# A fused attention and expert layer on one core: new order at the start, tanh for sigmoid, packed shared rows, attention added on GpSimd

## What is computed

```python
x = x + layernorm(attn(layernorm(x), W_basis, W_v, b_v, W_o, b_o))
x = x + layernorm(ffn(layernorm(x), gate_w, gate_bias, Wg, Wu, Wd, Sg, Su, Sd))

def attn(h):
    latent = h @ W_basis.T                       # queries and keys are the same, R = 64
    v = h @ W_v.T + b_v
    att = softmax(causal(latent @ latent.T / sqrt(R)))
    return (att @ v) @ W_o.T + b_o

def ffn(x):
    scores = sigmoid(x @ gate_w.T)               # 64 experts in 8 groups
    choice = scores + gate_bias                  # 4 groups by their two best, then the top 8
    rw = 2.5 * chosen scores / their sum
    routed = sum over e of rw[:, e] * ((silu(x @ Wg[e].T) * (x @ Wu[e].T)) @ Wd[e].T)
    shared = (silu(x @ Sg.T) * (x @ Su.T)) @ Sd.T   # 176 rows
    return routed + shared
```

## Time and profile before

| what | us |
|---|---|
| median of three runs (lowest, highest) | 492.09 (491.2, 492.85) |
| the profiled execution | 490.94 |
| its span | 489.1 |
| busy in it: PE, PEld | 453.5, 368.0 |
| busy in it: DVE, ACT, POOL | 331.1, 292.3, 340.8 |

### The profile page before, as it was taken

One profiled execution on the slowest core, in us unless ns is written; L12 is line 12 of the kernel. 1 busy time (PEld: TensorE's weight loads), 2 busy tenths in 40 slices (PEclk: granted clock), 3 DMA queues, 4 the chain that ended last, 5 costly groups with the idle time before them and its releaser, 6 DMA issues.

```text
span 489.1 us, 8048 instructions
## 1 busy us (share of the span) xinstructions
PE 453.5 (93%) x2144; PEld 368.0 (75%) x2144; DVE 331.1 (68%) x712; ACT 292.3 (60%) x570; POOL 340.8 (70%) x324
## 2 busy tenths in 40 slices
PE   0799886889999999999999999999999999999994
PEld 0598774658677888888888888888888888887894
DVE  4466798778556666666666666666666666666786
ACT  1478988665656555655555565655555556555652
POOL 6473556767468767677777777777777776778675
PEclk9999999799999999999999999999999999999998
DMA  7000000100001101010000101010101010100011
GB/s 199 1 2 2 17 18 0 33 2 0 1 16 35 33 17 32 17 30 18 20 29 16 32 16 32 16 32 16 32 16 32 16 32 16 28 4 0 0 45 43
DMA packets 12297, 11.58 MB, mean 24 GB/s; under 512 B 1734, under 2 KB 12278, under 8 KB 12278
## 3 DMA queue, kind: packets, MB, share of 16 engines
q1 hardware_dynamic: 11414, 11.02, 7.9%
q10 hardware_dynamic: 864, 0.33, 0.3%
HBM read 10.30 MB, written 1.05 MB: 23 GB/s over the span
## 4 chain that ended last, share of the span: by engine, by line
PE 82%; POOL 5%; DVE 4%; issue 4%; ACT 3%; DMA 1%; ACTq 0%; POOLq 0%; DVEq 0%
PE ps L1257 24%; PE ps L1259 24%; PE ps L1258 24%; POOL lat_hi L510 3%; PE ps L1209 3%; PE ps L1195 1%; DMA bo_sb<-in_b_o 1%; PE ps L1147 1%; PE ps L1155 1%; PE ps L1393 1%; PE ps L1175 1%; PE ps L1176 1%; PE ps L1252 1%; ACT L691 1%; POOL rstd L487 0%
## 5 line engine op out<-in xcount | busy, mean ns | idle before, releaser
L510 POOL TENSOR_TENSOR lat_hi<-hid,lat_hl 128x512 fp32r<-128x512 f32 (+1 forms) x188 | 241.2, 1285 | 101.9 <-ACT lat_hl L729 101.5
L960 DVE TENSOR_TENSOR up_w<-ps,route_w 128x512 f32<-128x512 f32 (+1 forms) x180 | 122.2, 679 | 107.8 <-PE ps L1259 107.6
L719 ACT ACTIVATE ps<-ps 128x512 f32<-128x512 f32 (+1 forms) x180 | 103.0, 573 | 132.8 <-PE ps L1259 132.3
L1257 PE MATMUL ps<-x_hi,w_hi 128*128 128x512 f32 (+1 forms) x360 | 141.0, 392 | 3.5 <-POOL w_lo L518 2.0
L1259 PE MATMUL ps<-x_hi,w_lo 128*128 128x512 f32 (+1 forms) x360 | 140.4, 390 | 0.0
L1258 PE MATMUL ps<-x_lo,w_hi 128*128 128x512 f32 (+1 forms) x360 | 140.1, 389 | 0.0
L970 DVE TENSOR_TENSOR hid<-ps,up_w 128x512 f32<-128x512 f32 (+1 forms) x180 | 122.4, 680 | 11.1 <-ACT ps L719 2.9
L729 ACT CAST lat_hl<-hid 128x512 fp32r<-128x512 f32 (+1 forms) x188 | 113.6, 605 | 16.0 <-DVE hid L970 12.6
L1257 PEld LDWEIGHTS ps<-x_hi,w_hi 128*128 128x128 f32 x360 | 67.8, 188 | 20.1 <-POOL w_lo L518 2.4
L1259 PEld LDWEIGHTS ps<-x_hi,w_lo 128*128 128x128 f32 x360 | 67.9, 189 | 14.8
L1258 PEld LDWEIGHTS ps<-x_lo,w_hi 128*128 128x128 f32 x360 | 67.9, 189 | 14.3
(11 more groups left out here) (132 smaller groups left out, 387.2 us busy)
## 6 DMA issues: line engine op xcount, KB each, us to landing
w_raw<-in_w_experts SPq DMA_DIRECT2D x44, 192.0 KB, 2.4
x_sb<-in_x SPq DMA_DIRECT2D x3, 256.0 KB, 6.0
out<-x_sb SPq DMA_DIRECT2D x3, 256.0 KB, 2.3
sh_raw<-in_w_shared_up SPq DMA_DIRECT2D x2, 88.0 KB
x_sb<-in_x ACTq DMA_DIRECT2D x2, 64.0 KB, 2.3
x_sb<-in_x SPq DMA_DIRECT2D x2, 64.0 KB, 2.1
out<-x_sb SPq DMA_DIRECT2D x1, 128.0 KB, 1.8
out<-x_sb SPq DMA_DIRECT2D x2, 64.0 KB, 1.6
```

Of the source, the lines that this page charges most:

```text
L510: g.tensor_tensor(hid_lo[:, k % DEEP, 0:w], hid[:, k % 2, 0:w], hid_hi[:, k % DEEP, 0:w], ALU.subtract).then_inc(s_hlo, 1)
L719: a.activation(bank, bank, ACT.Silu).then_inc(s_gated, 1)
L960: v.tensor_tensor(up_w[:, k % 2, 0:w], ps[:, gate_bank(k) + 1, 0:w], route_w[:, group, 512 * q + lo:512 * q + lo + w], ALU.mult).then_inc( ...
L1257: t_.matmul(out_, hi, mhi, start=start, stop=False)
```

## The change

- Orders: all eight lists are new. At the start the first transposes and the latent of quad 0 come before the weight product K0 (PE and ACT), P0 comes right behind S0 on DVE, and the centring is in two parts: B0 for the output weights, which waits for three transfers, and B1 for the bias, which has a semaphore of its own. PE begins with ten products of the identity with itself. POOL makes the select tables (B0) behind P1.
- SP loads gate weights and bias between x quads 1 and 2.
- Shared rows: the 176 rows are cut 128 + 48 instead of 88 + 88. The second step keeps up and gate in one weight block, the gate columns from 64 on, so that three products give both (`rest_gate_up`); seven transfers instead of four, and a memset of the gap.
- Sigmoid is Tanh with scale 0.5 on ACT, and DVE turns it into 0.5 * t + 0.5 (F on DVE) before POOL's bias sum.
- `add_attention` moves from DVE (four fused instructions) to POOL (a product with the root broadcast, then a sum, each over the whole quad).
- The picked scores come in one DVE pass: (left == TAKEN) * scores; keep_experts and POOL's weigh_scores go.
- In the tail DVE makes the last low hidden part (W20), and ACT takes the square root of the last unit's variance (Y4, with a Sqrt of a constant column before it, P0); DVE inverts it in N4.

Left out below: the new semaphores, the helpers that count steps and waits (`ups_through`, `is_rest`), the copies of the packed weights in L on ACT and POOL (now 384 columns in one for c = 0, and 112 columns plus 48 rows for c = 1), the row counts handed to Z and W, and the dispatch of stages.

```diff
-            "K0 P0 Q0 V0 P1 A00 A01 A02 Q1 T00 T02 A03 C00 T04 C01 T06 A10 C02 C03 A11 T10 T11 "
-            "V1 A12 T12 P2 C10 A13 T13 Q2 C11 T14 P3 V2 A20 T15 Q3 T16 T17 C12 C13 A21 W0 E0 "
-            "A22 T20 V3 F0 A23 T22 C20 A30 T24 A31 C21 T26 A32 T30 C22 T31 C23 T32 C30 T33 E1 "
-            "A33 T34 C31 T35 F1 T36 T37 G0 W1 Z0 C32 N00 C33 E2 F2 Z1 Z2 N01 Z3 G1 W2 Z4 W3 E3 "
-            "W4 F3 Z5 Z6 N10 W5 N11 G2 Z7 W6 W7 N20 Z8 Z9 W8 N21 Z10 Z11 W9 Z12 Z13 W10 W11 "
-            "Z14 W12 W13 Z15 W14 G3 Z16 N30 W15 W16 Z17 Z18 N31 W17 W18 Z19 Z20 W19 W20 Z21 "
-            "Z22 W21 W22 Z23 "
+            "P0 Q0 K0 V0 A00 P1 A01 T00 Q1 A02 A03 T02 C00 T04 C01 T06 A10 C02 C03 A11 W0 T10 "
+            "T11 A12 V1 P2 A13 T12 C10 T13 Q2 C11 P3 V2 A20 T14 T15 Q3 T16 T17 C12 T20 C13 A21 "
+            "E0 A22 V3 F0 A23 C20 T22 T24 A30 C21 T26 C22 A31 T30 C23 T31 A32 T32 T33 A33 C30 "
+            "E1 T34 F1 C31 T35 T36 G0 Z0 T37 C32 N00 E2 C33 F2 W1 Z1 N01 Z2 G1 Z3 W2 Z4 E3 W3 "
+            "Z5 W4 F3 Z6 N10 N11 G2 W5 Z7 W6 W7 N20 Z8 W8 N21 Z9 Z10 Z11 W9 Z12 Z13 W10 Z14 "
+            "W11 W12 W13 Z15 G3 Z16 W14 N30 W15 W16 Z17 Z18 N31 W17 W18 Z19 W19 Z20 Z21 W20 "
+            "W21 Z22 W22 Z23 "
         )
         ACT_ORDER = stages(
-            "P0 K0 Q0 P1 A00 A01 T00 Q1 A02 T02 A03 T04 C01 T06 R0 A10 C03 T10 A11 T12 A12 P2 "
-            "L0 Q2 C11 P3 T14 A13 Q3 T16 A20 Y0 C13 E0 F0 A21 T20 A22 T22 A23 T24 A30 C21 T26 "
-            "A31 T30 R1 C23 Y1 A32 T32 L1 E1 T34 A33 F1 T36 G0 C31 Z0 Y2 N00 E2 C33 Z1 F2 N01 "
-            "Z2 G1 W0 Z3 W1 R2 R3 W2 Y3 Z4 W3 E3 F3 Z5 W4 Z6 N10 N11 W5 G2 Z7 W6 N20 W7 Z8 Z9 "
-            "W8 N21 Z10 W9 Z11 W10 W11 Z12 Z13 W12 W13 Z14 Z15 W14 G3 W15 Z16 N30 Z17 W16 Z18 "
-            "W17 N31 Z19 W18 Z20 W19 Z21 W20 Z22 W21 R4 Z23 W22 R5 "
+            "P0 Q0 K0 A00 P1 A01 T00 Q1 A02 T02 A03 T04 C01 T06 A10 C03 A11 T10 P2 T12 A12 R0 "
+            "L0 L1 Q2 C11 A13 P3 T14 A20 Q3 T16 T20 Y0 C13 E0 A21 F0 A22 T22 A23 C21 T24 A30 "
+            "T26 R1 T30 C23 A31 Y1 A32 T32 E1 T34 F1 A33 C31 Z0 T36 G0 Y2 N00 E2 F2 C33 Z1 N01 "
+            "Z2 R2 W0 W1 Z3 G1 R3 Y3 W2 E3 Z4 W3 W4 Z5 F3 Z6 N10 N11 W5 G2 W6 Z7 N20 Z8 W7 N21 "
+            "W8 Z9 Z10 W9 Z11 W10 W11 Z12 Z13 W12 W13 Z14 Z15 G3 Z16 W14 W15 N30 W16 Z17 Z18 "
+            "W17 N31 W18 Z19 W19 Z20 Z21 W20 W21 Z22 R4 Z23 W22 R5 "
         )
         DVE_ORDER = stages(
-            "S0 S1 B0 P0 K0 V0 Q0 A00 A01 S2 A02 A03 Q1 S3 A10 A11 V1 T11 A12 U0 T13 A13 Q2 X0 "
-            "T15 V2 A20 T17 Q3 A21 A22 U1 V3 A23 H0 A30 X1 A31 J0 T31 A32 I0 T33 O0 M0 A33 U2 "
-            "T35 X2 T37 G0 H1 J1 Z0 I1 O1 Z1 M1 U3 H2 X3 Z2 J2 Z3 G1 I2 O2 Z4 Z5 M2 Z6 G2 Z7 "
-            "H3 Z8 Z9 J3 Z10 Z11 I3 Z12 O3 Z13 M3 Z14 Z15 G3 Z16 Z17 Z18 Z19 Z20 Z21 Z22 Z23 "
+            "S0 P0 B0 S1 B1 K0 Q0 A00 V0 A01 S2 A02 A03 Q1 S3 A10 A11 T11 V1 A12 A13 T13 Q2 X0 "
+            "A20 T15 V2 T17 Q3 A21 V3 A22 F0 A23 H0 A30 X1 A31 J0 T31 A32 T33 I0 A33 O0 M0 F1 "
+            "T35 X2 T37 G0 H1 J1 Z0 I1 O1 F2 M1 Z1 H2 X3 Z2 J2 Z3 G1 I2 O2 Z4 Z5 M2 Z6 F3 G2 "
+            "Z7 H3 Z8 J3 Z9 Z10 Z11 Z12 Z13 I3 O3 M3 Z14 Z15 G3 Z16 Z17 Z18 Z19 Z20 Z21 Z22 "
+            "Z23 "
         )
         POOL_ORDER = stages(
-            "S0 S1 P1 S2 S3 P2 D0 P3 X0 L0 D1 F0 X1 J0 R0 D2 E0 O0 L1 M0 E1 R1 F1 X2 J1 E2 O1 "
-            "D3 F2 M1 W0 X3 R2 W1 W2 J2 R3 W3 F3 E3 O2 M2 W4 W5 W6 W7 W8 J3 W9 W10 W11 W12 O3 "
-            "W13 M3 W14 W15 W16 W17 W18 W19 W20 W21 R4 W22 R5 "
+            "S0 S1 P1 B0 S2 S3 P2 P3 D0 U0 R0 L0 X0 D1 U1 F0 X1 D2 R1 J0 E0 L1 U2 M0 E1 F1 X2 "
+            "J1 E2 D3 F2 U3 M1 R2 W0 W1 X3 J2 R3 W2 W3 W4 M2 W5 F3 W6 W7 W8 W9 J3 W10 W11 E3 "
+            "W12 M3 W13 W14 W15 W16 W17 W18 W19 W20 W21 R4 W22 R5 "
...
-            "D0 Z0 D1 D2 Z1 Z2 D3 Z3 Z4 D4 Z5 D5 Z6 D6 Z7 Z8 D7 Z9 T0 Z10 D8 D9 D10 Z11 D11 "
-            "Z12 T1 Z13 Z14 D12 D13 D14 Z15 Z16 T2 Z17 D15 D16 Z18 Z19 D17 D18 D19 T3 D20 D21 "
-            "D22 T4 "
+            "D0 Z0 D1 Z1 D2 Z2 D3 Z3 Z4 D4 D5 Z5 D6 Z6 Z7 T0 Z8 D7 D8 Z9 Z10 D9 D10 Z11 T1 Z12 "
+            "D11 D12 D13 Z13 Z14 D14 Z15 Z16 T2 D15 D16 Z17 D17 D18 Z18 Z19 T3 D19 D20 D21 D22 "
+            "T4 "
         )
         ACT_TAIL = stages(
-            "W0 R2 Z0 W1 R3 Z1 Z2 W2 W3 Z3 W4 Z4 W5 Z5 W6 Z6 W7 Z7 Z8 O0 W8 Z9 W9 Z10 W10 O1 "
-            "Z11 W11 Z12 W12 Z13 W13 Z14 W14 O2 Z15 Z16 W15 W16 Z17 W17 W18 Z18 Z19 O3 W19 W20 "
+            "R2 W0 Z0 W1 R3 Z1 Z2 W2 Z3 W3 W4 Z4 W5 Z5 W6 Z6 O0 Z7 W7 W8 Z8 W9 Z9 W10 Z10 O1 "
+            "Z11 W11 Z12 W12 W13 Z13 Z14 W14 O2 W15 Z15 Z16 W16 Z17 W17 Z18 W18 Z19 O3 W19 W20 "
+            "P0 Y4 "
         )
         DVE_TAIL = stages(
-            "Z0 Z1 Z2 Z3 Z4 Z5 Z6 Z7 Z8 Z9 S0 Z10 N0 Z11 Z12 S1 Z13 Z14 N1 Z15 Z16 Z17 S2 Z18 "
-            "Z19 N2 S3 O4 S4 N3 N4 "
+            "Z0 Z1 Z2 Z3 Z4 Z5 Z6 Z7 S0 Z8 Z9 Z10 N0 Z11 Z12 S1 Z13 Z14 Z15 Z16 S2 Z17 N1 Z18 "
+            "Z19 S3 W20 O4 N2 S4 N3 N4 "
         )
         POOL_TAIL = stages(
-            "W0 R2 W1 R3 W2 W3 W4 W5 W6 W7 W8 W9 Y0 W10 W11 W12 W13 Y1 W14 W15 W16 W17 W18 Y2 "
-            "W19 W20 Y3 Y4 "
+            "R2 W0 W1 R3 W2 W3 W4 W5 W6 W7 Y0 W8 W9 W10 W11 W12 W13 W14 W15 Y1 W16 W17 W18 W19 "
+            "Y2 Y3 "
...
-            for q in range(1, QUADS):
+            def load_quad(q):
                 sp.dma_start(x_sb[:, 4 * q:4 * q + 4, :],
                              x_tiles[:, 4 * q:4 * q + 4, :]).then_inc(s_x[q], 16)
+
+            load_quad(1)
             sp.dma_start(gw_sb[:], gate_w_t).then_inc(s_gwl, 16)
             sp.dma_start(gb_sb[:], gate_bias.to_broadcast([P, E])).then_inc(s_gwl, 16)
-            for c in range(SHARED):
-                sp.dma_start(sh_raw[:, c, 0:2 * SROWS], w_shared_up[c]).then_inc(s_shl, 16)
-                sp.dma_start(sh_raw[0:SROWS, c, WD:WD + P], w_shared_down[c]).then_inc(s_shl, 16)
+            load_quad(2)
+            load_quad(3)
+            own = P - SROWS
+            ups = [w_shared_up[c].rearrange("h (g n) -> h g n", g=2) for c in range(SHARED)]
+            full = sh_raw[:, 0, 0:WD].rearrange("p (g n) -> p g n", g=2)
+            sp.dma_start(full[:, :, 0:SROWS], ups[0]).then_inc(s_shl, 16)
+            sp.dma_start(full[:, :, SROWS:P], ups[1][:, :, 0:own]).then_inc(s_shl, 16)
+            sp.dma_start(sh_raw[0:SROWS, 0, WD:WD + P], w_shared_down[0]).then_inc(s_shl, 16)
+            sp.dma_start(sh_raw[SROWS:P, 0, WD:WD + P],
+                         w_shared_down[1, 0:own]).then_inc(s_shl, 16)
+            sp.dma_start(sh_raw[:, 1, 0:REST], ups[1][:, 1, own:SROWS]).then_inc(s_shl, 16)
+            sp.dma_start(sh_raw[:, 1, GATE_AT:GATE_AT + REST],
+                         ups[1][:, 0, own:SROWS]).then_inc(s_shl, 16)
+            sp.dma_start(sh_raw[0:REST, 1, WD:WD + P],
+                         w_shared_down[1, own:SROWS]).then_inc(s_shl, 16)
...
+            g.memset(eps_col[:], EPS).then_inc(s_eps, 1)
+            g.memset(sh_raw[:, 1, REST:GATE_AT], 0.0).then_inc(s_gap, 1)
...
+            def add_attention(q):
+
+                k = 2 + q % 2
+                own = x1_sb[:, 4 * q:4 * q + 4, :]
+                pool.wait_ge(s_rstd, NORMS.index(("D", q)) + 1)
+                link(g.tensor_tensor(own, att[:, q % 2],
+                                     rstd[:, k].unsqueeze(2).to_broadcast([P, 4, C]), ALU.mult))
+                g.tensor_tensor(own, own, x_sb[:, 4 * q:4 * q + 4, :], ALU.add).then_inc(s_x1, 1)
...
-            def weigh_scores(q):
-
-                pool.wait_ge(s_kept, q + 1)
-                g.tensor_tensor(left[:], left[:], scores[:, q % 2], ALU.mult).then_inc(s_picked, 1)
...
-                    if (what, q) == ("S", 1):
-                        make_select()
...
-                             ACT.Sigmoid).then_inc(s_sc, 1)
+                             ACT.Tanh, scale=0.5).then_inc(s_sc, 1)
...
+                if is_rest(s):
+                    a.activation(gated[0:REST, k % 2, :], ps[GATE_AT:GATE_AT + REST, gate_bank(k), :],
+                                 ACT.Silu).then_inc(s_gated, 1)
...
+                elif what == "P":
+
+                    act.wait_ge(s_eps, 1)
+                    a.activation(deviation[:, 2:3], eps_col[:], ACT.Sqrt)
+                elif what == "Y":
+                    act.wait_ge(s_var, len(VARIANCES) + k + 1)
+                    a.activation(deviation[:, 0:2], mv[:, 2 + k % 2, 0:2, 1], ACT.Sqrt,
+                                 bias=eps_col[:]).then_inc(s_dev, 1)
...
-            def add_attention(q):
-
-                k = 2 + q % 2
-                dve.wait_ge(s_rstd, NORMS.index(("D", q)) + 1)
-                for t in range(4):
-                    ins = v.scalar_tensor_tensor(
-                        out=x1_sb[:, 4 * q + t, :], in0=att[:, q % 2, t, 0:C],
-                        scalar=rstd[:, k, t:t + 1], in1=x_sb[:, 4 * q + t, :],
-                        op0=ALU.mult, op1=ALU.add)
-                ins.then_inc(s_x1, 1)
...
+            def sigmoid_of_tanh(q):
+
```

(78 more changed lines are left out.)

107 lines of the change are left out of this document (66 added, 41 removed).

## The result

The kernel after takes 485.03 us, median of 4 runs (483.34 to 485.48), against 492.47 for the kernel before beside it: ratio 0.9848, 95% interval 0.9817 to 0.9879. It is 7.4 us faster. The forecast was 475.6 us, range 469.0 to 482.5; the result lies outside it, at less than half of the forecast gain. The profiled run took 483.34 us, 1.84 us more than its span as before, so the traces differ by 7.6 us, and can be compared term by term. It is the fastest of the four, 1.7 us under their median.

The account below looks back on a forecast made before the run. TensorE was taken to bind the loop from 147 to 442 us, so gains come only from the start, gaps to 147 us, fewer matmuls and the tail. Terms summed to 16.5 us: 492.09 - 16.5 = 475.6 us, range 469 to 482.5.

Parts of the forecast that it names:

- additions: Attention added on POOL: 1.5 us gained by relieving DVE, 1.5 us charged for POOL's fuller queue.
- The start: New order up to A01, with P1 as the limit and ten warming matmuls: 5.4 us gained, bounds 3.5 and 7.2.
- Tanh 1.8 us: Sigmoid by tanh drops table loads, ending TensorE's wait for exp_rows: 1.8 us gained, bounds 0 and 2.6.
- rival (c): Tanh is not in Silu's set, so four table loads stay in the middle: 478.2 us, chance 0.06.
- The middle: 75 to 94 us: half of 7.7 us of idle and slow-clock time goes, 4.0 us, bounds -3 and 7.7.
- rival (a): The middle keeps its gaps under another owner, POOL's pairs replacing DVE's pieces and table loads: 480.6 us, chance 0.25.
- Packing: Shared rows cut 128+48 save 12 matmuls of 0.231 us: 2.8 us, lower bound 1.4 if half falls into gaps.
- 94 to 147 us: Of 3.8 us TensorE idles from 94.2 to 147 us, 1.0 us goes, bounds 0 and 3.8.
- The tail: Shorter last root and earlier D22, less 0.35 us for N2's scalings: 1.5 us gained, bounds 0.5 and 2.5.
- 0.95 us for D22: In the tail, W19 ahead of the fourth root and W20 on DVE start D22 up to 1.3 us sooner; 0.95 taken.

Follow-up runs that it names:

- after_again: The kernel after, unchanged, measured once more in five rounds on one chip: 485.44 us (483.34 to 487.8).
- no_warm: The kernel after without the ten start matmuls that nobody reads: 485.82 us (484.88 to 486.46).
- rest_doubled: The kernel after with the packed gate-and-up products of each quad's 48 shared rows issued twice, 12 matmuls more: 487.22 us (484.76 to 488.56).
- the probe: The kernel after plus 18 VectorE instructions behind its end, alone, then beside a GpSimd train: five with both inputs in SBUF took 5.40 instead of 1.59 us.
- u3_dve: The kernel after with only quad 3's attention addition moved from GpSimd back to VectorE: 481.55 us, repeated 484.18 us.

## Why the prediction was wrong

The direction was right and the size not: 16.5 us were forecast and 7.4 came, 7.6 in the traces. To share these out one needs places in TensorE's list that have the same stages ahead of them in both kernels. A01, the logits of quad 2 (F2), N20 and the first step of the rounds are such places (20.33, 74.39, 98.15 and 142.79 us before; 14.55, 68.61, 92.20 and 135.93 after).

```profile
74.39 1.08 PE L1228 MATMUL ps<-gw_sb,x_t 128*128 128x64 f32 x8 [0.77 <-ACT x_t L684]
```

In the kernel after:

```profile
68.61 1.00 PE L1292 MATMUL ps<-gw_sb,x_t 128*128 128x64 f32 x8
```

| TensorE's work | gained, us | forecast, us |
|---|---|---|
| up to A01 | 5.8 | 5.4 |
| A01 to F2 | 0.0 | 1.8 (tanh), 1.5 - 1.5 (additions) |
| F2 to N20 | 0.2 | 4.0 (middle), 0.7 (3 packed matmuls) |
| N20 to the rounds | 0.9 | 1.0 (gaps), 2.1 (9 packed matmuls) |
| the tail | 0.7 | 1.5 |

- **The start, 5.4 us: right.** P1's transposes are at 14.16 (14.2 to 14.7 forecast) and A01 at 14.55 instead of 20.33, 5.8 us. But this trace has the best start; after_again's is 1.1 us worse at quad 2. Typical is 4.7.

```profile
8.90 1.13 PE L1211 MATMUL ps<-xn_t,wb_sb 128*128 128x512 f32 x2 [0.68 <-ACT xn_t L671]
...
14.16 0.63 PE L1175 MATMUL ps<-ident,xn 128*128 128x128 f32 x4 [1.24 <-POOL xn L575]
14.55 0.36 PE L1239 MATMUL ps<-lat_hi,lat_hl 128*128 128x256 f32 x1
```

The latent pair takes 1.13 instead of 2.07 us after the ten extra products; no_warm says how little of it reached the end.

- **Tanh 1.8 us: nothing of it between A01 and F2,** which are 54.06 us apart in both kernels. Taken back there alone it costs 1.7 us, and the additions 2.7, so both have a worth in the new order, but the order as a whole gained nothing over the old one here. Three table loads are left, as said, and rival (c) is out:

```profile
L671 ACT ACT_TABLE_LOAD x1 | 1.3, 1283 | 3.6 <-issue 3.6
L774 ACT ACT_TABLE_LOAD x1 | 1.3, 1283 | 0.0
L848 ACT ACT_TABLE_LOAD x1 | 1.3, 1283 | 0.0
```

- **The middle, 4.0 us: this step failed, the largest of the misses.** The busy times from F2 to N20, before and after:

```profile
74.39:98.15 23.76, 17.15 (x72) 12.76 (x72) 17.94 (x70) 18.18 (x34) 16.97 (x19) 0.86 0.06 17
```

```profile
68.61:92.20 23.59, 16.98 (x70) 12.04 (x69) 21.91 (x76) 12.58 (x29) 17.33 (x19) 0.86 0.06 18
```

TensorE idles 6.6 us in both and has the same mean clock: no gap closed, each only changed its owner, and the three packed matmuls are lost in the wait at N01. This is rival (a)'s picture. In after_again the same stretch takes 25.78 us, 2.0 us longer than before, at a clock of 0.74 from 75 to 95 us. I took half of the gaps as closed because the table loads vanish and GpSimd had idle time. GpSimd's idle time was what let H2 run in 2.2 us. Rival (a) named the mechanism, the lock between GpSimd and two-input VectorE instructions, and gave 480.6 us at 0.25; that too was 4.4 us low, as it kept the full tanh, packing and tail terms. I weighed the lock only as a slower add (0.53 us where two took 0.61) and not as a chain of eleven instructions of 0.2 us with a whole GpSimd instruction in front of each of six. That is 5.4 us on VectorE, of which 3.6 reached TensorE. The wait of 2.3 us at N01, from the new order and not from the lock, was not foreseen either. What was tried on the lock gave back 1.3 to 3.5 us of a miss of 9.4: it is shown as a cause, and as a part of the miss only.
- **The clock.** From 84.5 to 94.2 us it is 0.87 instead of 0.65, but 0.86 instead of 1.00 in the stretch ahead. In every trace of the new order with a wait of TensorE of 2.8 to 3.8 us in this stretch it fell behind that wait, whoever was awaited, so a wait of 3.6 us costs more than itself: behind it the matmuls come 0.43 us apart from 83.7 to 85 us instead of 0.23. Behind waits of 2.0 to 2.4 us it fell in some traces and not in others.
- **Packing, 2.8 us: 1.75.** The page has 2152 matmuls against 2144, which is 12 fewer and 20 extra ones at the start (ten products, two instructions each). By rest_doubled the nine behind N20 are worth 1.75 us and the three ahead of it nothing. The lower bound of 1.4 allowed for matmuls that fall into gaps; the sum took none.
- **94 to 147 us, 1.0 us: wrong.** From N20 to the rounds 0.9 us were gained, less than the nine matmuls alone are worth, so the gaps there cost about 0.8 us more than before.
- **The tail, 1.5 us: 0.7.** From the aggregate's end (478.05) to the last scaling's start is 0.63 us, as forecast, and 0.9 us are gained:

```profile
475.91 0.42 DVE L1111 TENSOR_TENSOR y_t<-ps,y_t 128x256 f32<-128x256 f32 x1 [0.71 <-PE ps L1323]
476.25 1.11 DVE L1134 SCALAR_TENSOR_TENSOR x_sb<-ps,rstd,x_sb 128x128 f32<-128x128 f32 x4
477.28 0.48 DVE L876 BATCH_NORM_STATS2 stats<-ps 128x6 f32<-128x128 f32 x2
477.80 0.25 DVE L879 BATCH_NORM_AGGREGATE mv<-stats 128x2 f32<-128x6 f32 x2
...
478.68 0.61 DVE L1134 SCALAR_TENSOR_TENSOR x_sb<-ps,rstd,x_sb 128x128 f32<-128x128 f32 x2
```

The 0.95 us for D22 was wrong: it starts at 475.25 instead of 482.13, just the 6.9 us of the loop. Before, its low parts ended at 482.08 on GpSimd; now the chain of hidden products ahead of it ends as late, and only the engine of the last subtraction has changed. N2 cost 0.2 us (TensorE's T4 ended at 477.10, S4 began at 477.28).

The deeper fault is the adding up. Taken from the kernel after, tanh is worth 3.5 us, the additions on GpSimd 2.4, packing 2 (of these only tanh's is clear of the scatter); put into the kernel before, tanh is worth nothing. My reading, which no run isolates, is that each order of stages fits its set of durations, so that a part alone finds it misfitted. A sum of terms read from the old trace assumes the old order's slack. Not settled is which part of the new order pays for the old: the head on the old order already lost 1.8 of its 4.2 us by 71 us, and no run separated the order of the other stages from the edits.

## What to carry to other kernels

Work given to GpSimd is paid by VectorE too, wherever short instructions with two SBUF inputs (or a tensor_scalar within SBUF) run beside it: price it as one GpSimd instruction for each of them, look for their inflated lengths (1.1 us where 0.2 is usual) rather than for waits, and place such chains where GpSimd idles or keep one input in PSUM (only the probe tried the latter). When a stretch is passed between three engines, a gap removed from one of them can come back under another owner: here it did at 2 to 4 us in six orders tried, and in three of them TensorE's clock fell behind the wait. Count a lead only at places that have the same stages ahead of them in both orders. Compare such variants in medians of several runs: here one comparison gave 3.5 us and its repetition 1.3.

## What the runs showed that I had not expected

- tensor_scalar within SBUF is held as much as a two-input instruction: 0.25 to 1.05 us each. With one input in PSUM 0.32 us stay 0.32, and GpSimd's train kept 1.07 us a piece.
- The granted clock from 12 to 20 us differs from run to run under the same instructions (1.00, 0.79, 0.59), and quad 2's transposes come up to 2.1 us later with it; a chain that just fits between two GpSimd instructions then fits or not.
- A hand-over through one more engine (ScalarE, VectorE, GpSimd in place of ScalarE, GpSimd) cost nothing clear by its 0.29 us (492.05 against 491.64) and 4.1 us by where it stood in VectorE's queue.
- u3_dve had the lowest median, but with its repetition it isn't clearly ahead of the kernel after. Its two comparisons with the kernel before give 0.9784 (0.9735 to 0.9834) and 0.985 (0.9823 to 0.9878).
